# Attention row sums: two accumulating transfers per half beside GpSimd's quad add, and one round of summing matmuls in place of three

## The reference, cut to what matters

```
attn = jnp.einsum('bhqd,bhkd->bhqk', query, key) / scale
attn = jax.nn.softmax(attn, axis=-1)
out = jnp.einsum('bhqk,bhkd->bhqd', attn, value)
```

## Time and profile before

| | |
|---|---|
| median of 3 runs | 3239.81 us (3238.47 to 3241.17) |
| the profiled execution's own time | 3239.41 us |
| its span | 3237.6 us, so 1.8 us lie around it |
| busy in the span | PE 96%, DVE 68%, POOL 63%, ACT 46% |
| mean granted TensorE clock | 0.981 |

### The profile page before, as it was taken

How to read it: one execution, slowest core, us unless ns; L and a number is a source line. 1 busy time by engine, 2 the same in 40 slices (tenths; PEclk the granted TensorE clock), 3 DMA queues, 4 the chain that set the end, 5 groups by cost and what they waited for, 6 DMA issues and landing times. The chain is left out here.

```text
span 3237.6 us, 43860 instructions
## 1 busy us (share of the span) xinstructions
PE 3097.1 (96%) x16020; PEld 2049.8 (63%) x16020; DVE 2201.2 (68%) x3337; ACT 1487.9 (46%) x2714; POOL 2034.4 (63%) x654
## 2 busy tenths in 40 slices
PE   7999999989999999999999999999975999999998
PEld 4888888855555555555555555555524778777876
DVE  3555445567777777777777777777718777887784
ACT  1222122226666666666666666666652232233232
POOL 0111112127888888888888888888874566666663
PEclk8999999989999999999999999999987999999999
DMA  3454544652424242424242423333115133233221
GB/s 102 157 188 162 175 167 164 188 144 56 102 57 102 57 102 57 102 57 102 61 100 63 96 68 90 74 85 78 35 49 147 53 105 104 61 95 104 83 73 40
DMA packets 179855, 315.79 MB, mean 98 GB/s; under 512 B 16081, under 2 KB 52081, under 8 KB 179697
## 3 DMA queue, kind: packets, MB, share of 16 engines
q1 hardware_dynamic: 179696, 313.70, 35.1%
HBM read 194.59 MB, written 118.49 MB: 97 GB/s over the span
## 5 line engine op out<-in xcount | busy, mean ns | idle before, releaser
L280 DVE TENSOR_REDUCE part_max<-ps_m 128x1 f32<-128x512 f32 x1984 | 1211.8, 681 | 415.3 <-PE ps_m L264 415.3
L911 POOL TENSOR_TENSOR pairs<-probs 128x2048 f32<-128x2048 f32 x256 | 1169.3, 4577 | 307.3 <-ACT probs L892 302.2
L892 ACT ACTIVATE probs<-ps_s 128x512 f32<-128x512 f32 x2048 | 1036.8, 624 | 429.4 <-PE ps_s L804 357.9
L264 PE MATMUL ps_m<-k_stack,q_stack 96*128 96x512 f32 x1984 | 817.2, 413 | 40.3 <-DVE neg_max L277 34.2
L804 PE MATMUL ps_s<-q_stack,k_stack 97*128 97x512 f32 x2048 | 818.3, 402 | 6.2 <-PEq L313 4.1
L264 PEld LDWEIGHTS ps_m<-k_stack,q_stack 96*128 96x128 f32 x1984 | 377.1, 190 | 307.8 <-DVE part_max L280 136.0
L817 PE MATMUL ps_o<-probs,v_tiles 128*32 128x512 f32 x4096 | 494.8, 601 | 0.0
L804 PEld LDWEIGHTS ps_s<-q_stack,k_stack 97*128 97x128 f32 x2048 | 387.9, 190 | 136.7 <-ACT probs L892 21.7
L548 POOL TENSOR_TENSOR y_cos<-y_rot,cos 64x512 f32<-64x512 f32 x16 | 20.5, 1283 | 475.6 <-DVE y_swap L644 475.6
L915 POOL TENSOR_TENSOR pairs<-pairs 128x2048 f32<-128x2048 f32 x64 | 293.1, 4579 | 5.0
L817 PEld LDWEIGHTS ps_o<-probs,v_tiles 128*32 128x32 f32 x4096 | 107.3, 109 | 233.6 <-issue 177.0
(11 more groups left out here) (178 smaller groups left out, 4748.8 us busy)
## 6 DMA issues: line engine op xcount, KB each, us to landing
q_stack<-q_hi_scratch SPq DMA_DIRECT2D x128, 256.0 KB, 5.8
k_stack<-k_hi_scratch SPq DMA_DIRECT2D x64, 512.0 KB, 10.3
x_in<-in_x SPq DMA_DIRECT2D x16, 1024.0 KB, 5.5
q_hi_scratch<-st_hi SPq DMA_DIRECT2D x64, 256.0 KB, 2.3
q_lo_scratch<-st_lo SPq DMA_DIRECT2D x64, 256.0 KB, 2.5
k_hi_scratch<-st_hi SPq DMA_DIRECT2D x64, 256.0 KB, 2.4
k_lo_scratch<-st_lo SPq DMA_DIRECT2D x64, 256.0 KB, 2.7
v_scratch<-st_v SPq DMA_DIRECT2D x64, 256.0 KB, 2.3
```

Source lines behind the costliest of these rows:

```text
L264: nc.tensor.matmul(bank[:, :], att["q"][r][0:ROWS, half, h, q * P:(q + 1) * P], att["k"][r][0:ROWS, h, kc * CH:(kc + 1) * CH], start=True, ...
L280: nc.vector.reduce_max(part_max[:, half, j, kc:kc + 1], bank[:, :], AX).then_inc(att["m_read"], 1)
L892: nc.scalar.activation(probs[:, (r * UNITS + u) % PR, x // HG, x % HG, :], ps_s[place(u * UT + x) % SR][:, :], ACT.Exp, scale=SCALE).then_ ...
L911: nc.gpsimd.tensor_tensor(pairs[:, w, :, :], probs[:, (r * UNITS + u) % PR, 0, :, :], probs[:, (r * UNITS + u) % PR, 1, :, :], ALU.add).th ...
```

## The change

GpSimd still makes four pair adds and one quad add per half. The quad add moves from behind unit 1 to behind unit 3 and adds `pairs[2]` to `pairs[3]`. Two transfers that GpSimd issues do the rest: the first, behind unit 1's pair add, adds `pairs[0]` to `pairs[1]`; the second, behind the quad add, adds `pairs[1]` to `pairs[3]`. Both are SBUF to SBUF, 1 MB, with `accum_op=ALU.add`, and count up `joined`. TensorE then sums only `pairs[3]`, in one round of four matmuls, and this round and its copy stand two units later in TensorE's and ScalarE's streams than before (`L_AT` is the place in the bank ring). The second transfer is issued only once the first has landed. The pair adds of units 0 and 1 wait for the transfers of the half before, since these still read or write the slots.

```
--- before.py
+++ after.py
@@ -683,12 +683,11 @@
     TILES = UNITS * UT
     SR = 3
     PR = 3
-    ADDED = [1, 2, 4, 5]
     ADDS = ROUNDS + 1
-    SUMMED = [1, 2, 3]
+    SUMMED = [3]
     SUMS = len(SUMMED)
     RUN = TILES + NQ
-    L_AT = UT
+    L_AT = 3 * UT
     HALF_RUN = ROUNDS * UT + 1
     assert RUN % SR == 0 and R3 * UNITS % PR == 0
 
@@ -730,6 +729,7 @@
         exped = sem("exped")
         pv_done = sem("pv_done")
         pair_done = sem("pair_done")
+        joined = sem("joined")
         sum_done = sem("sum_done")
         o_out = sem("o_out")
         o_stored = [sem(f"o_stored{q}") for q in range(NQ)]
@@ -823,7 +823,7 @@
                 v = l_place(n, qc)
                 pe.wait_ge(exped, taken(n, v - SR))
                 for k, w in enumerate(SUMMED):
-                    pe.wait_ge(pair_done, (n * NQ + qc) * ADDS + k + 3)
+                    pe.wait_ge(joined, 32 * (n * NQ + qc + 1))
                     for a in range(HG):
                         m = nc.tensor.matmul(ps_s[v % SR][a * HD:(a + 1) * HD, :], ones[:, :], pairs[:, w, a, :],
                                              start=k == 0, stop=k == SUMS - 1)
@@ -847,11 +847,12 @@
                         scores(n, r, u, x)
                     if u >= 1:
                         pv(n, i, r, u - 1)
-                        if u == ROUNDS:
+                        if u == ROUNDS + 2:
                             sums(n, 0)
+                        if u == 2 and not is_first(n):
+                            sums(n - 1, 1)
                     elif not is_first(n):
                         pv(n - 1, i if r else i - 1, (r - 1) % R3, UNITS - 1)
-                        sums(n - 1, 1)
                     maxima(spread[u][UT])
                 if is_last(n):
                     pv(n, i, r, UNITS - 1)
@@ -879,14 +880,16 @@
                 for u in range(UNITS):
                     if u == ROUNDS + 1:
                         take_o(n, 0)
+                    if u == ROUNDS + 3:
                         take_l(n, 0)
                     if u == 1 and not is_first(n):
                         take_o(n - 1, 1)
+                    if u == 3 and not is_first(n):
                         take_l(n - 1, 1)
                     if u >= PR or not is_first(n):
                         act.wait_ge(pv_done, n * UNITS + u - PR + 1)
                         qc, w = divmod(u - PR, ROUNDS)
-                        act.wait_ge(pair_done, (n * NQ + qc) * ADDS + ADDED[w])
+                        act.wait_ge(pair_done, (n * NQ + qc) * ADDS + w + 1)
                     for x in range(UT):
                         act.wait_ge(scored, n * TILES + u * UT + x + 1)
                         nc.scalar.activation(probs[:, (r * UNITS + u) % PR, x // HG, x % HG, :], ps_s[place(u * UT + x) % SR][:, :],
@@ -902,18 +905,29 @@
             def step(i, r, n):
                 for u in range(UNITS):
                     qc, w = divmod(u, ROUNDS)
+                    h = n * NQ + qc
                     if not (is_first(n) and qc == 0):
                         if w == 0:
-                            pool.wait_ge(pair_done, (n * NQ + qc) * ADDS)
+                            pool.wait_ge(joined, 32 * h - 16)
+                        elif w == 1:
+                            pool.wait_ge(joined, 32 * h)
+                        elif w == 2:
+                            pool.wait_ge(pair_done, h * ADDS)
                         else:
-                            pool.wait_ge(sum_done, (n * NQ + qc - 1) * SUMS + w)
+                            pool.wait_ge(sum_done, h * SUMS)
                     pool.wait_ge(exped, taken(n, place(u * UT + UT - 1)))
                     nc.gpsimd.tensor_tensor(pairs[:, w, :, :], probs[:, (r * UNITS + u) % PR, 0, :, :], probs[:, (r * UNITS + u) % PR, 1, :, :],
                                             ALU.add).then_inc(pair_done, 1)
                     if w == 1:
-                        pool.wait_ge(pair_done, (n * NQ + qc) * ADDS + 2)
-                        nc.gpsimd.tensor_tensor(pairs[:, 1, :, :], pairs[:, 0, :, :], pairs[:, 1, :, :],
+                        pool.wait_ge(pair_done, h * ADDS + 2)
+                        nc.gpsimd.dma_start(pairs[:, 1, :, :], pairs[:, 0, :, :], accum_op=ALU.add).then_inc(joined, 16)
+                    if w == 3:
+                        pool.wait_ge(pair_done, h * ADDS + 4)
+                        nc.gpsimd.tensor_tensor(pairs[:, 3, :, :], pairs[:, 2, :, :], pairs[:, 3, :, :],
                                                 ALU.add).then_inc(pair_done, 1)
+                        pool.wait_ge(pair_done, h * ADDS + 5)
+                        pool.wait_ge(joined, 32 * h + 16)
+                        nc.gpsimd.dma_start(pairs[:, 3, :, :], pairs[:, 1, :, :], accum_op=ALU.add).then_inc(joined, 16)
 
             rounds(step)
```

8 lines of the change are left out of this document (4 added, 4 removed).

## The result

The changed kernel takes 3483.3 us (median of 4 runs, 3480.5 to 3488.5) against 3239.1 for the kernel before: a ratio of 1.0757, with a 95% interval of 1.0741 to 1.0773, so 244 us slower. The forecast was 3445 us, in a range of 3230 to 3760.

A forecast was written before the change was run, and what follows sets the result against it. TensorE was taken to bound the old kernel, GpSimd's loop with its transfer wait the changed one. 3239.4 + 64 x (29.8 - 26.67) = +200, + 9 gave 3449, stated as 3445 us; range 3230 to 3760.

The forecast's parts named there:

- 19.4 + D: GpSimd's loop from landing to landing: four adds, one issue at 1.0 us, handovers and the flight make a half.
- D: Time from the second transfer's issue start to its landing: 8.7 us outside the loads, 12.1 inside, mean 10.4.
- The gain on TensorE: TensorE's sum round drops 16 of 24 rows: 1.84 us less per half, 118 us over 64 halves.
- my half way: Second transfer inside the loads' burst: delay taken halfway between no sharing cost and fair sharing, +3.4 us.
- Sharing fairly would double its 6.7 us of data time: Second transfer inside the group's loads: upper case for the delay, from equal sharing of the DMA engines.
- TensorE's wait and the clock: TensorE at its sum round: some 5 us wait per half, low clock possible afterwards, hidden by GpSimd's own 10.2 us.
- that rival: TensorE's low clock lasts 14 us after each wait, so TensorE sets the time: 3530 us, chance 0.08.
- The first transfer: Before L930: its flight of 8.7 us is hidden under 13.7 us of pair adds and quad add.
- The small transfers behind the stores: SP's queue: row-maximum transfers stand behind sum stores that move two units later; costed at nothing.
- The end of the stage: After the last adds: uncovered issue and flight, 9.7 us, less 0.5 for fewer matmuls; taken as 9 us.
- The quick transfer: Rival: second read hides behind the write, halves of 25.0 to 25.4 us, 3155 us; mean D under 7.2, chance 0.12.
- The chain of two transfers: Rival: D over 13.7 us delays L930, half becomes 4.6 + 2D; 3892 us at D = 16, chance 0.13.

The follow-up runs named there:

- the split loads: On top of the slot twice and loads issued after the second transfer's landing, each group's loads are issued in two parts: 3175.0 us, ratio 0.9794.
- the slot twice: Changed kernel with a fifth `pairs` slot, so unit 1's pair add waits for a transfer of two halves ago: 3367.9 us, ratio 1.039.

## Why the prediction was right, point by point

- **The bound and the loop.** GpSimd's loop through the wait before unit 1's pair add is what sets a half. Put at 19.4 + D, measured 19.85 + D. The 0.45 us are the issues: an issue takes 0.61 us from its start to the next add and 0.30 us of waiting before it, and the two adds behind it take 0.25 us more than others (9.41 us against 2 x 4.58), 1.2 us in all where I took 1.0; and the loop holds the first issue whole and the 0.30 us before the second. Over 64 halves this term is 29 us. The mean flight, 10.8 in this loop where I put 10.4, is another 25, and together they are more than the 34 between 3449, the sum, and 3483: the halves at both ends of the attention, which I put like all others, give 20 back. That it is this wait and not the work, the run without transfers and the split loads show; that it is this slot, the fall of the short halves from 27.0 to 25.4 with the slot twice.
- **The gain on TensorE.** Put at 1.84 us a half; without transfers it is 26.66 - 25.0 = 1.7.
- **The flight, D.** The mean came out right (10.4 put, 10.5 to the landing and 10.8 to the next add measured) by two errors against each other, and that is luck. Outside the loads I put 8.7 and it is 7.0: the slope of stores to HBM, 3.33 us per MB and read, was too slow inside SBUF, where the data of such a transfer take 4.8 us in all and not 6.7. Inside the loads I put 12.1 and it is 13.9. An estimate with the measured 7.0 and 4.8 of data, and my half way (+2.4) inside the loads, would have been a mean of 8.2 and some 3305 us, about 180 under the time measured. That an accumulating transfer pays its data time twice held: a packet of 8 KB takes 0.64 us with the addition and 0.33 without (medians of the packets outside the burst). That this is the second read and not an adding unit at half the rate is not shown; both would give these times. By the Trainium skill (DMA: Bandwidth & Descriptors, section Anatomy of one DMA, with the two reads of Collectives: The Full Stack, section on the bandwidth ceiling) an estimate of 6.8 us came out; the trace agrees within 0.3.
- **Sharing with the loads.** Which flight would meet the burst was right: the loads start 13.5 us after a landing (1595.96 to 1609.48) where I put about 12. The step that failed is the size of what the loads cost, "Sharing fairly would double its 6.7 us of data time": a plain copy, with half the data time, and a transfer of half the size still take 13.0 and 11.9 us there. The packets of the two queues show why (q0 is GpSimd's, q1 SP's; the windows are a first transfer alone, then the second one issued at 1615.83):

```profile
q0 software_dynamic: 144, 1.05, 74.6%
```

```profile
q1 hardware_dynamic: 544, 1.36, 106.7%
```

```profile
q0 software_dynamic: 144, 1.05, 70.1%
q1 hardware_dynamic: 194, 0.73, 32.5%
```

  They are the queues' lines of 1600.8 to 1607.8, of 1615.8 to 1621.9 and of 1621.9 to 1629.1 us: packets, MB, and the time of the packets that start there as a share of the 16 engines' time. For the first 6.1 us in the burst the DMA engines serve loads only and not one packet of the transfer; then it takes some 7 us beside the rest of the loads. Over the halves that meet the burst, the medians of the first data packet's start are 6.7 us after the issue for the second transfer, 6.3 for the plain copy and 6.6 for half the size, against 1.5, 1.2 and 1.5 outside it. From there to the last packet's end pass 6.4, 5.6 and 4.2 us, against 5.2, 3.2 and 2.8. So most of what the burst adds is a late start of some 5 us that does not depend on the transfer's size. The flight does not last until the burst is through: the group's last load lands a median of 2.1 us after it (1.1 to 3.9). The loads meanwhile lose little: the medians of the last two of a group go from 12.9 and 13.9 us to 16.8 and 17.4 in the changed kernel. Why the transfer starts late was not tried.
- **TensorE's wait and the clock.** Put: 5 us of wait in every half; measured: 8.6 us in every other one. Put further: a return of TensorE's branch within 9.4 us at the low level, hidden by GpSimd's own 10.2. Measured: the branch takes 8.4 us in the run with the slot twice, and in the changed kernel GpSimd's pair adds wait 3.1 us in 1000 for ScalarE. After its 8.48 us wait TensorE's matmuls come at the low level:

```profile
1567.95 1.93 PE L828 MATMUL ps_s<-pairs,ones 128*32 128x512 f32 x8 [8.48 <-DMA pairs<-pairs]
...
1573.39 0.63 PE L264 MATMUL ps_m<-k_stack,q_stack 96*128 96x512 f32 x1
...
1574.23 0.41 PE L264 MATMUL ps_m<-k_stack,q_stack 96*128 96x512 f32 x1
```

  for 6.3 us, and in the short halves, whose sum round follows without a wait, not at all. It recovers here as in the earlier trace rows; by the granted clock the low level lasts 3.2 to 8.9 us from the start of the sum rounds that were waited for in mid-attention, never the 14 of that rival, which falls. Where I was careless is in what opens when GpSimd's wait is taken away: the slot by itself left the long halves to this branch, and that run came 100 us above what I expected of it.
- **The first transfer.** Hidden, as put: no wait for a DMA stands before L930. Its cover is 15.0 us (1600.85 to 1615.83), not 13.7, since the issue itself and the waits around both issues count too.
- **The small transfers behind the stores.** Nothing, as put: `pairs` is the only tile whose DMA an engine waits for from 1000 to 2000 us.
- **The end of the stage.** Put at 9: the last quad add ends at 2645.60, the sum round starts at 2652.99 and takes 1.93, so 9.3 us, against 1.1 from the last add to the end of the last round before: 8.2 us are added.
- **The rivals.** The quick transfer needed a mean flight under 7.2 us. Outside the loads the flight is in fact 7.0, which with the loop as measured gives halves of 26.9 us and would leave the kernel about even; the loads decided it. The chain of two transfers needed a first flight over 13.7 us, in truth over 15.0; the first transfers never met the loads and took 9.2 us at most in mid-attention. The adding rate that this rival supposed, under 4 bytes in a ns on each engine, is far off: 8 KB in 0.64 us are 12.8.

## What to carry to other kernels

A transfer that replaces arithmetic is hidden only as far as the first later instruction that reuses its source or its destination: follow each engine's stream from the issue to that instruction, count what stands between, and compare with the flight beside the other traffic, not with the flight alone. Here one add (4.9 us) stood there against flights of 7 to 14 us. Extra room for the one slot that is reused first, and moving the bulk loads to where a covered transfer flies, turned a loss of 7.6% into a gain of 2.1%; asking for one transfer in place of two gave 1.7% without either.

## What the runs showed of the hardware that I had not expected

- Issuing a transfer from GpSimd costs about 1.2 us of its time: 0.30 before it, 0.61 from its start to the next add, and the two adds behind it take 0.25 us more. The profile's row says 0.88 us and overlaps the add behind it. The plain copy's row is 0.60 us.
- An accumulating SBUF to SBUF transfer of 1 MB lands 7.0 us after its issue, a plain one after 4.7, one of 512 KB that accumulates after 4.6 (medians). In a burst of loads from another queue these become 13.9, 13.0 and 11.9: the burst adds 6.9, 8.4 and 7.3 us, no less for the small ones, and some 5 of them pass before the first data packet starts.
- GpSimd's adds and TensorE's matmuls are not slowed by the traffic: with a DMA share of 0.73, in the run with the split loads, where it was 0.34, five adds and two issues still take 25.3 us, and the means of TensorE's matmul rows in that window are 598 and 397 ns for `pv` and the scores, as before.
